# Expert loop with 39 written-out blocks, a buffer for each group in the last stage, and a smaller clearing

## The reference

```python
x = x + layernorm(attn_block(layernorm(x)))   # linear ("performer") attention, 16 heads, then a GELU MLP
x = x + layernorm(ffn_block(layernorm(x)))    # mixture of experts
```

```python
shared = silu(x @ shared_w1.T) @ shared_w2.T
top_k_gates, top_k_idx = top_k(x @ gate_w.T, 2)
gates = softmax(top_k_gates)
selected = sum over the 2 experts of gate * (silu(x @ w1[e]) @ w2[e])
out = shared + selected
```

## Time and profile before

| | |
|---|---|
| median of 3 runs | 632.97 us (631.84 to 634.09) |
| profiled execution, its own time | 631.46 us |
| span from its first to its last instruction | 629.7 us |
| mean granted TensorE clock | 0.895 |
| TensorE busy | 484.4 us, 77% |
| VectorE / ScalarE / GpSimd busy | 329.9 / 245.6 / 274.0 us |
| experts' loop, first transpose to last matmul | 440.8 to 581.1 us |
| last stage, from there to the end | 48.6 us |

### The profile page before, as it was taken

One profiled execution on the slowest core, in us unless ns is written; L12 is line 12 of the kernel. 1 busy time (PEld: TensorE's weight loads), 2 busy tenths in 40 slices (PEclk: granted clock), 3 DMA queues, 4 the chain that ended last, 5 costly groups with the idle time before them and its releaser, 6 DMA issues.

```text
span 629.7 us, 11204 instructions
## 1 busy us (share of the span) xinstructions
PE 484.4 (77%) x3423; PEld 352.0 (56%) x3424; DVE 329.9 (52%) x1327; ACT 245.6 (39%) x482; POOL 274.0 (44%) x380
## 2 busy tenths in 40 slices
PE   4699998699578699999789956920999999999000
PEld 2456653456447456664436635620799898998000
DVE  5878551549896386672245989530233232322272
ACT  3344433234334344443225335310454444543043
POOL 7400000116756555000001775775266566666593
PEclk9699998899889999999769979985899999999655
DMA  8810000000002321000000000142222222221681
GB/s 290 313 48 1 1 2 1 0 1 1 2 1 69 97 68 40 1 2 2 1 0 1 1 2 17 61 138 70 73 82 87 77 77 68 85 73 43 184 293 70
DMA packets 26781, 38.39 MB, mean 61 GB/s; under 512 B 4464, under 2 KB 19184, under 8 KB 26480
## 3 DMA queue, kind: packets, MB, share of 16 engines
q1 hardware_dynamic: 20976, 26.15, 13.3%
q0 software_dynamic: 4608, 9.58, 4.5%
q10 hardware_dynamic: 1152, 2.10, 0.9%
HBM read 21.88 MB, written 15.93 MB: 60 GB/s over the span
## 4 chain that ended last, share of the span: by engine, by line
PE 58%; DVE 19%; POOL 8%; issue 7%; ACT 4%; DMA 3%; POOLq 0%; ACTq 0%; SPq 0%; DVEq 0%
PE pQKV L887 6%; PE pPQ L887 6%; PE pF L754 4%; DVE MID L1122 4%; PE pF L616 4%; DVE st L1112 3%; PE pQKV L845 3%; PE pKV L690 3%; POOL xs L505 3%; PE pPK L616 3%; PE pF L618 3%; PE pF L617 3%; PE pPK L618 3%; PE pPK L617 3%; PE pF L705 2%
## 5 line engine op out<-in xcount | busy, mean ns | idle before, releaser
L444 POOL TENSOR_TENSOR ve<-mv,eps 128x4 f32<-128x4 f32 x40 | 8.0, 201 | 233.9 <-DVE mv L1116 233.9
L578 POOL DMA_INDIRECT ys<-MID,PQT x80 | 77.6, 971 | 31.1 <-issue 30.8
L505 POOL DMA_INDIRECT xs<-PL,SLOT x64 | 62.0, 968 | 18.4 <-issue 18.1
L448 POOL TENSOR_TENSOR rs<-ve,halves 128x4 f32<-128x4 f32 x40 | 40.7, 1018 | 3.1
L887 PE MATMUL pPQ<-E,HT 128*128 x320 | 39.7, 277 | 1.0 <-ACT HT L1060 0.5
L887 PE MATMUL pQKV<-E,HT 128*128 x320 | 39.7, 277 | 0.0
L1024 ACT ACTIVATE HT<-pPK,wunscale 128x512 f32<-128x512 f32 x32 | 21.1, 687 | 47.0 <-PE pPK L618 47.0
L887 PEld LDWEIGHTS pPQ<-E,HT 128*128 128x128 f32 x320 | 37.3, 192 | 2.3 <-issue 1.7
L887 PEld LDWEIGHTS pQKV<-E,HT 128*128 128x128 f32 x320 | 37.3, 192 | 1.6 <-issue 1.3
L1012 ACT ACTIVATE HT<-pPK,cols_s 128x512 f32<-128x512 f32 x32 | 22.0, 687 | 40.9 <-PE pPK L791 40.2
L1415 DVE TENSOR_SCALAR MID<-pPQ,PQT 128x128 f32<-128x128 f32 x40 | 12.3, 346 | 47.2 <-PE pPQ L887 47.1
(11 more groups left out here) (245 smaller groups left out, 1264.3 us busy)
## 6 DMA issues: line engine op xcount, KB each, us to landing
PQT<-xs SPq DMA_DIRECT2D x40, 132.0 KB, 2.1
MID<-ys SPq DMA_DIRECT2D x8, 512.0 KB, 4.2
PQT<-in_ew1T SPq DMA_DIRECT2D x1, 2304.0 KB, 9.9
E<-in_ew2T SPq DMA_DIRECT2D x1, 2304.0 KB, 10.3
X<-in_x SPq DMA_DIRECT2D x8, 256.0 KB, 6.1
HT<-in_ew1T SPq DMA_DIRECT2D x8, 256.0 KB, 4.1
sh<-PK SPq DMA_DIRECT2D x8, 256.0 KB, 2.7
PK<-sh SPq DMA_DIRECT2D x8, 256.0 KB, 4.8
```

Of the source, the lines that this page charges most:

```text
L448: eng.tensor_tensor(rs[:, j, g, :], ve[:, j, g, :], halves[:], ALU.pow).then_inc(s_rs[j], 1)
L505: eng.indirect_dma_start(xs, bass.IndirectOffsetOnAxis(SLOT[:, g, t, a:a + 1], 0), PL[:, g, t, a, :], None).then_inc(s_scat[g], 16)
L578: eng.indirect_dma_start(ys, bass.IndirectOffsetOnAxis(XS[q][:, t, ID_AT:ID_AT + 1].bitcast(U32), 0), Y[q][:, t, :], None).then_inc(s_ysc[ ...
```

## The change

- NBLK is 39, and SPARE, the number of spare rows, falls from 2048 to 1792. Their clearing in xs takes two DMAs instead of four.
- The MEMSET of PL covers only words 128 to 131 of each row.
- On all engines the blocks are written out; the expert's number is read into a register once a block, before the waits, and kept for `down_block`. The dummy transpose of the last block goes.
- In the last stage each group has buffers of its own: SUM (the shared results, in the second half of PQT), YC (in PQT, MID and E2), OUT (in HT and XN). The loads of SUM are issued by SyncE in the experts' loop, after block 7's load. The eight loads of YC are issued one after the other when all scatters have landed. The sum is made in place in SUM, the routed sum in place in YC, the result in OUT.
- `root5` adds eps, takes the power, multiplies the mean by it and then negates.

```diff
-NBLK = -(-(TOPK * B * S // BW + E - 1) // UNROLL) * UNROLL
+NBLK = TOPK * B * S // BW + E - 1
...
-        YC = [mid[:, 0:2 * GW], mid[:, 2 * GW:4 * GW]]
+        half = pq[:, 4 * 2 * GW:]
+        SUM = list(parts(half, *[GW] * NG))
+        YC = list(parts(pq, *[2 * GW] * 4)) + list(parts(mid, *[2 * GW] * 2)) + list(
+            parts(E2[:].rearrange("p e c d -> p (e c d)"), *[2 * GW] * 2))
...
-        OUT = [XN[:, 2, :], XN[:, 3, :]]
+        OUT = [v[:, i, :] for v in (HT, XN) for i in range(4)]
...
-            for g in range(GB):
-                n = SPARE // GB
+            for g in range(2):
+                n = SPARE // 2
...
-            load_blocks(0)
-            with sp.Fori(1, NBLK // UNROLL) as j:
-                load_blocks(j)
+            for k in range(NBLK):
+                q = k % UNROLL
+                row = sp.value_load(ROW[0:1, k:k + 1], min_val=0, max_val=XROWS - BW)
+
+                wait(sp, s_ysc[q], k // UNROLL * 32)
+                sp.dma_start(XS[q], xs[bass.ds(row, BW)].rearrange("(p a) w -> p a w", a=2)).then_inc(s_bx[q], 16)
+                if k == UNROLL - 1:
+                    for h in range(2):
+                        sp.wait_ge(s_shst[h], 16 * (NG // 2))
+                    for n in range(NG):
+                        sp.dma_start(SUM[n], sh[n]).then_inc(s_shl, 16)
 
             for q in range(UNROLL):
-                sp.wait_ge(s_ysc[q], 32 * (NBLK // UNROLL))
...
+                sp.wait_ge(s_ysc[q], 32 * len(range(q, NBLK, UNROLL)))
+
+            for n in range(NG):
+                sp.dma_start(YC[n], ys_v[n]).then_inc(s_bx[n], 16)
...
-            eng.memset(PL[:], 0.0).then_inc(s_free, 1)
+            eng.memset(PL[:].rearrange("p g t a w -> p (g t a) w")[:, :, D:RW], 0.0).then_inc(s_free, 1)
...
+            def root5(n):
                 pool.wait_ge(s_mv5, n + 1)
-                eng.tensor_tensor(mm5[:, q], zeros[:], mv5[:, q, :, 0], ALU.subtract)
...
+                eng.tensor_tensor(ve5[:, n], mv5[:, n, :, 1], eps[:, 0, :], ALU.add).then_inc(s_ve5, 1)
+                pool.wait_ge(s_ve5, 3 * n + 1)
+                eng.tensor_tensor(rs5[:, n], ve5[:, n], halves[:], ALU.pow).then_inc(s_ve5, 1)
+                pool.wait_ge(s_ve5, 3 * n + 2)
+                eng.tensor_tensor(nm5[:, n], mv5[:, n, :, 0], rs5[:, n], ALU.mult).then_inc(s_ve5, 1)
+                pool.wait_ge(s_ve5, 3 * n + 3)
+                eng.tensor_tensor(nm5[:, n], zeros[:], nm5[:, n], ALU.subtract).then_inc(s_nm5, 1)
+
+            add_routed(0)
+            add_routed(1)
+            for n in range(NG):
+                root5(n)
+                if n + 2 < NG:
+                    add_routed(n + 2)
...
+            turn_block(0)
+            last = None
+            for k in range(NBLK):
+                ew = pe.value_load(EW[0:1, k:k + 1], min_val=0, max_val=E)
+
+                wait(pe, s_si, 2 * k - 2)
+                pe.wait_ge(s_bl, k + 1)
+                if k + 1 < NBLK:
+                    turn_block(k + 1)
+                up_block(k, ew)
+                if k:
+                    down_block(k - 1, last)
+                last = ew
+            down_block(NBLK - 1, last)
...
+            dve.wait_ge(s_shl, 16 * NG)
+            for n in range(NG + 1):
+                if n < NG:
+                    sum_stats(n)
+                if n:
+                    residual(n - 1)
```

More of the change, by code:

```diff
@@ L570, in _ @@
             send_rows(B - 1, GB - 1)
[L573 to L579, removed]
@@ L910, in _ @@
-            turn_block(0, 0)
-            blocks(0, False)
-            with pe.Fori(1, NBLK // UNROLL - 1) as j:
-                blocks(j, False)
-            j = NBLK // UNROLL - 1
-            blocks(j, True)
-            down_block(j, UNROLL - 1, weights_of(j, UNROLL - 1))
+            turn_block(0)
+            last = None
+            for k in range(NBLK):
+                ew = pe.value_load(EW[0:1, k:k + 1], min_val=0, max_val=E)
[7 more added lines that the diff above has]
+                last = ew
@@ L1041, in _, with hi_block @@
             banks = [pF[0], pF[1], pPK[0], pPK[1]]
[L1043 to L1044 removed]
+            def hi_block(k):
                 wait(act, s_u, 2 * k - 2)
                 act.wait_ge(s_bT, k + 1)
[L1047 to L1060 removed]
@@ L1062, in _ @@
-            hi_block(0, 0)
-            blocks(0, False)
-            with act.Fori(1, NBLK // UNROLL - 1) as j:
-                blocks(j, False)
-            blocks(NBLK // UNROLL - 1, True)
-            def norm_sum(i, q):
-                n = i * 2 + q
-                wait(act, s_out, n - 1)
+                A(XBH[:, k % 2, :], (pT, pKV)[k % 2][:, 0:BW], ACT.Copy).then_inc(s_bh, 1)
+            hi_block(0)
+            for k in range(NBLK):
+                if k + 1 < NBLK:
+                    hi_block(k + 1)
+                for h in range(2):
+                    if h == 0:
+                        wait(act, s_do, k - 1)
+                    act.wait_ge(s_u, 2 * k + h + 1)
+                    A(HT[:, k % 2 * 2 + h, :], banks[k % 2 * 2 + h][:], ACT.Silu, scale=wunscale[:]).then_inc(s_si, 1)
@@ L1082, in _, with store @@
-            norm_sum(0, 0)
-            norm_sum(0, 1)
-            store(0, 0)
-            with act.Fori(1, NG // 2) as i:
-                norm_sum(i, 0)
-                store(i - 1, 1)
-                norm_sum(i, 1)
-                store(i, 0)
-            store(NG // 2 - 1, 1)
-            for q in range(2):
-                act.wait_ge(s_st[q], 16 * (NG // 2))
+            def store(n):
+                act.wait_ge(s_out, n + 1)
+                act.dma_start(out_v[n], OUT[n]).then_inc(s_st, 16)
@@ L1095, in _ @@
+            norm_sum(0)
+            for n in range(1, NG):
+                norm_sum(n)
+                store(n - 1)
+            store(NG - 1)
+            act.wait_ge(s_st, 16 * NG)
         @block.vector
@@ L1430, in _ @@
-            lo_block(0, 0)
-            blocks(0, False)
-            with dve.Fori(1, NBLK // UNROLL - 1) as j:
-                blocks(j, False)
-            blocks(NBLK // UNROLL - 1, True)
-            result(NBLK // UNROLL - 1, UNROLL - 1)
-            def sum_stats(i, q):
-                n = i * 2 + q
+            lo_block(0)
+            for k in range(NBLK):
+                if k + 1 < NBLK:
+                    lo_block(k + 1)
+                if k:
+                    result(k - 1)
```

191 lines of the change are left out of this document (52 added, 139 removed).

## The result

The changed kernel takes 621.76 us (median of 4 runs, 621.10 to 623.00), the kernel before 632.99 us on the same chip (4 runs, 631.84 to 634.09). The ratio is 0.9825 [0.9802, 0.9848] at 95%: faster by 11.2 us. The forecast was 621.0 us.

The account below looks back on a forecast made before the run. TensorE was taken to bound the kernel, GpSimd to pace the tail. Gains 2.8 + 0.7 + 3.3 + 3.7 + 1.5 = 12.0 us gave 621.0 us on the median's scale, 8 in 10 for 616.0 to 626.5.

Parts of the forecast that it names:

- 7.0 (3.3 and 3.7): Experts' loop: 3.3 us from 39 blocks for 40, 3.7 us from writing out the Fori body (ends 0 and 3.81).
- The rival that the excess isn't the loop's: Experts' loop: writing out gains only 0 to 1.7 us, total 623.0 to 624.7 us; chance 12%.
- the back edges: Experts' loop: by the instruction-fetch rule alone only these come back, about 1.7 us with the slips beside them.
- the named danger: Start: the CAST falls behind the second MEMSET, ends at 22.4, and the clearing gains only 1.3 us.
- I take 2.8: Start: gain from the smaller clearing of PL, as TensorE's 2.85 us idle time goes; ends 1.3 and 2.9.
- The clock: Start: without the idle time TensorE's clock may rise earlier; worth 0 to 2.9 us, taken as 0.7.
- The next 30 us are TensorE's, so I let it pass to the end: Start: the 2.85 us of idle time saved by the clearing was carried through to the kernel's end.
- the early gain is lost again: Start: second MEMSET catches the CAST, or work waits at a later clock stretch; gain 0 to 1.3 us, chance 12%.
- the first group is ready at 596.0, 1.5 us earlier: Last stage: sum starts 0.9 us earlier, second add no longer delays the first root, 0.6; tail gains 1.5 us.
- GpSimd, not DMA, paces the tail: Last stage: loads running ahead are worth no more than the 1.5 us; groups come 3.31 us apart.
- the *slower* rival: Last stage: eight loads share the DMA engines, first add 10.7 to 17.2 us late, 631.7 to 638.2 us; chance 6%.
- The drain: fixed, as assumed: Span's end: GpSimd's 8.83 us drain keeps its length; if not, up to 3.9 us more may come back.

Follow-up runs that it names:

- run 2: Kernel before with only the loop written out, 39 blocks and 1792 spare rows; old clearing of PL and last stage: 672.23 us, ratio 0.9863 to the kernel before.
- run 1: Kernel before with only the smaller MEMSET of PL: 677.35 us, ratio 0.9978 to the kernel before.
- run 3: Changed kernel with 40 blocks, still written out: 674.72 us, ratio 0.9868 to the kernel before.
- run 4: Changed kernel with PL cleared in full again: 673.00 us, ratio 0.9908 to the kernel before.
- run 5: Changed kernel again with no edit: 621.94 us, ratio 0.9841 to the kernel before.
- run 8: Changed kernel with VectorE's sum of group n + 2 in front of the residual of group n: 624.31 us, ratio 0.9880 to the kernel before.
- run 9: Changed kernel with the root's mean negated first, as in the kernel before: 621.40 us, ratio 0.9835 to the kernel before.
- run 10: Changed kernel with roots of groups 0 to 5 in pairs and four adds ahead of the first root: 618.26 us, ratio 0.9790 to the kernel before.
- Run 6: Changed kernel with the spare rows' clearing moved behind the first batch's roots, its stores behind the first weight loads: 620.11 us, ratio 0.9797 to the kernel before.
- run 7: Changed kernel with the second add of routed results held until VectorE's first sum is done: 621.52 us, ratio 0.9825 to the kernel before.
- run 11: Changed kernel with each load of routed results held until the add two groups before is done: 661.87 us, ratio 0.9874 to the kernel before.

## Why the prediction was right, point by point

**The loop: right, shown.** The 35 periods average 3.315 us, TensorE is busy in all of them and no pause is left. 7.4 us came for 7.0 (3.3 and 3.7): one block of 3.31, so, by subtraction, writing out gave 4.1. That is 0.3 more than the excess worked out from the earlier trace rows, which was read from blocks 7 to 31 alone. The rival that the excess isn't the loop's (0 to 1.7) is refuted by the even periods, and run 2 agrees: its interval leaves out the block alone. Runs 1, 3 and 4 don't tell the two parts apart. The Trainium skill, page "Runtime: NRT & Kernel Launch", section "Instruction fetch mechanics", gives a taken branch that breaks the sequential prefetch as one reason why control flow is expensive. The prediction put the back edges at about 1.7 us with the slips beside them; the earlier trace rows shows 0.99 us of that. The trace gave 4.1, so more than the back edges was in it; whether that is the registers' arithmetic, as the prediction put it, was not tried by itself.

**The clearing: mechanism right, its size wrong by the named danger.** The step that failed is "I take 2.8". The second MEMSET caught the CAST: its end moved from 23.76 to 22.88, 0.9 us, and in runs 5, 8, 9 and 10 it ended between 22.57 and 22.73, 1.0 to 1.2 us earlier; the bound said 1.3. The prediction saw the MEMSET move up to 20.8 us and the CAST at 20.5, and trusted 0.3 us between two engines. It overlooked GpSimd's addition L542 between the MEMSETs, which met VectorE's addition of CC (0.50 us; 0.19 in run 4) and put the CAST off further. Run 6 is the term as forecast at the CAST, 23.76 - 20.98 = 2.8 us, but not at the loop, where 2.9 us are left of this term and the clock's together (forecast 3.5).

The long MEMSET didn't hold everything on VectorE. In the kernel before the addition of CC ran at its 0.19 us while the MEMSET was on, just before the CAST that was held:

```profile
20.28 0.19 DVE L1197 TENSOR_TENSOR CC<-MX,SS 128x32 f32<-128x32 f32 x1
```

The Trainium skill, page "SBUF — State Buffer", section "SBUF: two separate sides", has a rule with this distinction: whichever starts first, a GpSimd instruction or a VectorE instruction in a two-port mode, holds the shared ports for its whole instruction, while a VectorE instruction with two SBUF inputs meets only those GpSimd instructions that read SBUF. The traces agree: the CAST ends 0.04 us after either MEMSET, and the addition of CC takes 0.19 us beside the MEMSET, which reads nothing, but 0.50 beside the addition L542, which reads. That the CAST ran in such a mode no row shows.

**The clock: as forecast at first, then partly paid back.** 0.7 was taken for it; at 30 us it had added 1.3 (1.1 at the first transpose, 2.4 at the second). "The next 30 us are TensorE's, so I let it pass to the end" is the weaker step. The rival *the early gain is lost again* came half true: 2.4 us at 30 and at 97 us became 1.8 at the loop, in run 5 3.9 became 1.8, in run 6 5.4 became 2.9. The part that is lost by the fourth group goes with the clock of 100 to 130 us (the table in run 6). Why the low level comes when it does was not tried.

**The last stage: right in its bound, wrong in its gain.** Forecast 1.5 us, found 0.5. The step that failed is "the first group is ready at 596.0, 1.5 us earlier": after the last matmul's end its scale and bias are ready at 16.47 us, before at 16.40. The second add no longer stood before the root, but beside the first sum, which lost 1.0 us to it (run 7 gives 1.1 back). The first add itself came 0.2 us later after the loop (9.79 for 9.55), and the first root's addition took 0.56 us for 0.20 beside VectorE's second sum. The period was forecast at 3.31 us and is 3.34; 0.32 of it is again a meeting of the two engines. So the 0.5 us that came are 0.4 from the seven steps from first to last group (22.96 us for 23.37) and 0.2 from a shorter drain, less 0.1 at the first group. "GpSimd, not DMA, paces the tail" is shown by run 11, and the *slower* rival is refuted: the first load landed after 3.7 us, in its turn.

**The drain: fixed, as assumed.** 8.66 us with 39 blocks in all eleven traces, whatever the tail, 8.83 with 40 (8.82 in run 3). In the changed kernel it starts with GpSimd's last instruction and ends at 619.8, 3.8 us after ScalarE is done (616.0). In every trace GpSimd's last instruction sets the end like this, which is why run 10's shorter stage shows in the time.

The total was nearer than its parts, and that is luck. Start and last stage came 2.7 us short by the traces and the loop 0.4 over, so the traces give 9.7 us for a forecast of 12.0. The medians give 11.2 only because the profile of before lay 1.5 us under its median and that of after on it.

Two slips of the prediction changed nothing. Its least gain, 1.3 + 3.3 = 4.6 us, leaves out its own lower end of the tail, -1, and should have been 3.6 (629.4 us). And the last root of the kernel before took 1.56 us (at 619.03), not 1.4.

## What to carry to other kernels

A stall behind a long GpSimd instruction isn't gone when that instruction is; list what GpSimd runs next and whether VectorE's critical operation still falls beside it, to a tenth of a us. Where the two engines take turns in a small dependent chain, fewer and larger GpSimd instructions with the long adds made ahead of them shortened the stage by 3.7 us; changes of order alone gave from 2.3 us lost (run 8) to 1.1 us won (run 7). A loop body with addresses from registers can be priced by comparing its period with a written-out stretch of the same code.

## What the runs showed of the hardware

- GpSimd's MEMSET held VectorE's CAST (0.18 us alone) to its own end, for 3.25, 1.87 and 1.65 us, but not VectorE's addition of two inputs (0.19 us beside it; 0.50 beside GpSimd's addition).
- The conflict hits GpSimd's small operations too: 0.20 us became 0.37 to 0.73, a root of 1.02 us 1.36 or 1.50, each beside a VectorE operation with two inputs.
- A root of twice the words costs less than twice: 1.02 us for 4 words a partition, 1.67 for 8.
- Two of the three chips ran every kernel 6 to 8% slower, written-out or not, before and after. Their traces have pauses in which no engine waits for something of this kernel. The chain of run 1 at 195 to 215 us (start, length, what):

```profile
200.69 12.28 another core or an unknown queue
```

and TensorE in run 1 behind that pause:

```profile
213.79 0.61 PE L616 MATMUL pPK<-XFH,E1H 128*128 128x512 f16 x1 [6.09 <-issue]
```

In the loop of run 3 the written-out blocks have gaps too:

```profile
540.87 0.41 PE L851 MATMUL pKV<-ident,PQT 128*128 128x128 f32 x2 [0.51 <-ACT HT L1026]
```

That looks like engines waiting for their instructions, but it is only argued: what the pauses are was not tried. By the ratios, edits near the change are worth about as much there (0.9863 to 0.9908 in runs 2 to 4, 0.9874 in run 11) as on the first chip (0.9825 and 0.9841), while a difference of 2 us can't be told on them.
